# Experts' results added into one row per token by the sending transfers

## The reference

```python
h = _layernorm(x) * (1 + ca) + sa
x = x + ga * attention_stack(h)              # 4 layers, 16 heads of 8
h = _layernorm(x) * (1 + cb) + sb            # 4096 tokens
probs = softmax(h @ router_w + router_b)     # E = 16 experts
vals, idx = top_k(probs, 2); vals = vals / sum(vals)
pos = place of the pair among those of its expert; within = pos < C   # C = 640
expert_inputs[idx, pos] += h * within
expert_outputs = (silu(xe @ w_gate) * (xe @ w_up)) @ w_down           # F = 176
output = (expert_outputs[idx, pos] * vals * within).sum over the token's 2 pairs
x = x + gb * (h + shared_mlp(h) + output)
```

## Time and profile before

| | |
|---|---|
| median of three runs | 1048.8 us (1045.79 to 1053.61) |
| the profiled execution | 1059.5 us |
| its span, first to last instruction | 1057.7 us |
| TensorE busy | 866.6 us (82%) |
| GpSimd busy | 734.4 us (69%) |
| VectorE busy | 729.1 us (69%) |
| ScalarE busy | 561.4 us (53%) |
| GpSimd, five sends for each of 16 experts (L633) | 80 x 0.96 us |
| DMA moved | 115.19 MB |

### The profile page before, as it was taken

The page is one execution under the profiler, slowest core; times in us unless marked ns, Lnnn a source line. Parts: engine busy times, 40 slices in busy tenths (PEclk is TensorE's granted clock), DMA queues, the critical chain, the costliest instruction groups (busy, mean ns, idle before and its releaser), DMA issues.

```text
span 1057.7 us, 10906 instructions
## 1 busy us (share of the span) xinstructions
PE 866.6 (82%) x3053; PEld 429.0 (41%) x3053; DVE 729.1 (69%) x1317; ACT 561.4 (53%) x885; POOL 734.4 (69%) x636
## 2 busy tenths in 40 slices
PE   4389998998999899999999996686643897989750
PEld 2034443433444343444444442244321465666530
DVE  3679998898888889888989898475552432222216
ACT  5358876775767577768787885553311121222110
POOL 3899988997999877898989896436626015545550
PEclk9689999998999899999999998786666787888775
DMA  7835444644636535535353440211211013232317
GB/s 222 237 91 141 121 115 126 168 115 114 180 103 159 148 102 135 150 80 143 96 136 104 113 126 1 59 41 61 80 53 51 23 31 101 81 94 79 101 35 238
DMA packets 89673, 115.19 MB, mean 109 GB/s; under 512 B 12960, under 2 KB 47238, under 8 KB 89614
## 3 DMA queue, kind: packets, MB, share of 16 engines
q1 hardware_dynamic: 80672, 102.87, 35.7%
q0 software_dynamic: 4608, 9.51, 2.7%
q10 hardware_dynamic: 4334, 2.13, 0.7%
HBM read 22.02 MB, written 21.14 MB: 41 GB/s over the span
## 4 chain that ended last, share of the span: by engine, by line
PE 56%; issue 14%; DVE 10%; DMA 5%; POOL 5%; SPq 3%; ACT 3%; another core or an unknown queue 3%; DVEq 0%; POOLq 0%; ACTq 0%
PE ps L1149 7%; PE ps L642 6%; PE ps L1075 6%; PE ps L1170 4%; PE ps L1130 4%; PE ps L1136 4%; DVE wnum L1526 3%; PE ps L1102 3%; PE ps L1116 3%; PE ps L1110 2%; POOL kv L951 2%; PE ps L1100 2%; PE ps L1127 2%; DMA kv<-expert_in_scratch 2%
## 5 line engine op out<-in xcount | busy, mean ns | idle before, releaser
L951 POOL TENSOR_TENSOR kv<-kv,kT 128x1024 f32<-128x1024 f32 x128 | 306.3, 2394 | 63.4 <-DMA kv<-vT 46.6
L1520 DVE TENSOR_TENSOR_SCAN kvsum<-kv,ps 128x256 f32<-128x256 f32 x256 | 166.9, 673 | 9.9 <-POOL kv L956 9.9
L956 POOL TENSOR_TENSOR kv<-kv 128x512 f32<-128x512 f32 x128 | 165.9, 1307 | 0.0
L633 POOL DMA_INDIRECT pair_out_scratch<-kv,idx_y x80 | 76.8, 960 | 126.3 <-DVE kv L772 103.2
L1526 DVE TENSOR_TENSOR wnum<-kvsum,ps 128x1024 f32<-128x1024 f32 x128 | 154.2, 1204 | 1.0
L1149 PE MATMUL ps<-u,w 128*128 128x512 f32 x256 | 122.3, 600 | 1.5 <-issue 0.9
L1365 ACT ACTIVATE hT<-ps,bias_h 128x512 f32<-128x512 f32 x128 | 84.6, 690 | 36.8 <-PE ps L1149 36.8
L1075 PE MATMUL ps<-u,wqkv 128*128 128x512 f32 x192 | 96.7, 629 | 5.5 <-ACT u L1281 3.3
L1170 PE MATMUL ps<-wnum,gather_e 128*32 128x512 f32 x512 | 69.2, 613 | 14.0 <-DVE wnum L1526 7.5
L619 POOL DMA_INDIRECT expert_in_scratch<-wnum,scat_u x64 | 62.9, 983 | 20.4 <-issue 17.9
L1149 PEld LDWEIGHTS ps<-u,w 128*128 128x128 f32 x256 | 48.7, 192 | 63.9 <-issue 54.7
(11 more groups left out here) (243 smaller groups left out, 1693.9 us busy)
## 6 DMA issues: line engine op xcount, KB each, us to landing
kv<-vT SPq DMA_DIRECT2D x256, 256.0 KB, 4.3
expert_in_scratch<-room SPq DMA_DIRECT2D x16, 325.0 KB, 4.8
kv<-expert_in_scratch SPq DMA_DIRECT2D x16, 325.0 KB, 2.9
pair_out_scratch<-room SPq DMA_DIRECT2D x16, 256.0 KB, 4.5
wnum<-x SPq DMA_DIRECT2D x16, 256.0 KB, 2.8
kv<-pair_out_scratch SPq DMA_DIRECT2D x8, 512.0 KB, 4.3
x<-in_L_attn_x_dram SPq DMA_DIRECT2D x8, 256.0 KB, 4.3
mod<-mod_scratch SPq DMA_DIRECT2D x1, 2048.0 KB, 9.8
```

The lines of the kernel that those rows point to most:

```text
L633: pool.indirect_dma_start(out=y_dram, out_offset=bass.IndirectOffsetOnAxis(ap=idx_y[:, par, j:j + 1], axis=0), in_=yes[:, par, j * P:(j + ...
L951: pool.tensor_tensor(pair, pair, kT[:, par:par + 1, :].to_broadcast([P, 2, S]), ALU.mult).then_inc(kv_weighed, 1)
L956: pool.tensor_tensor(even_, even_, odd_, ALU.add).then_inc(kv_done, 1)
L1520: dve.tensor_tensor_scan(kvsum[:, i, 1:PAIRS + 1], kv[:, par, i, 0:PAIRS], ps_q[:, 0:PAIRS], 0.0, ALU.add, ALU.bypass).then_inc(kvsum_done, 1)
```

## The change

- `y_dram` has one row per token instead of two (4096), then the rows of the empty places. Both pairs of a token get the same row number: the two iotas make the same numbers, and the third starts at 4096.
- The sends of results are made with an addition (`compute_op=ALU.add`): a row is added to what the row in DRAM holds, zeros or the other expert's result.
- Before its five sends expert e waits on GpSimd until the sends of expert e-1 have landed (for e > 0). The two experts of a token are different, so within one expert's sends each token's row comes once.
- `clear` writes 128 KB instead of 256 KB of zeros a slot into `y_dram`.
- In the final mix the load is one row per token (256 KB), and VectorE multiplies and adds x; the sum of the two pairs is gone.

Everything else is as it was, two line numbers further down behind L632.

```diff
--- before.py
+++ after.py
@@ -52,9 +52,9 @@
 
     XW = D + 2
     xe_dram = nc.dram_tensor("expert_in_scratch", [ROWS + 2 * TOK, XW], F32, kind="Internal").ap()
-    y_dram = nc.dram_tensor("pair_out_scratch", [2 * TOK + ROWS, D], F32, kind="Internal").ap()
+    y_dram = nc.dram_tensor("pair_out_scratch", [TOK + ROWS, D], F32, kind="Internal").ap()
     xe_tiles = xe_dram[0:ROWS, :].rearrange("(e p j) d -> e p (j d)", e=E, p=P)
-    y_rows = y_dram[0:2 * TOK, :].rearrange("(b p r) d -> b p (r d)", b=B, p=P)
+    y_rows = y_dram[0:TOK, :].rearrange("(b p r) d -> b p (r d)", b=B, p=P)
 
     with ExitStack() as ctx:
         def sb(name, shape, dt=F32):
@@ -252,7 +252,7 @@
         hs = wnum_room[:, 0:RING * 2 * NT * XW].rearrange("p (r k n c) -> p r k n c", r=RING, k=2, n=NT)
         YES = TILES * D + 2 * CT * XW
         yes = kv_room[:, YES:YES + 2 * CAP].rearrange("p (a c) -> p a c", a=2)
-        ypair = kv_room[:, 0:TILES * D].rearrange("p (r k n d) -> p r k n d", r=4, k=2, d=D)
+        ysum = kv_room[:, 0:TILES * D // 2].rearrange("p (r n d) -> p r n d", r=4, d=D)
         GROUPS = ((0, 1), (1, 3), (3, 5), (5, 7), (7, 8))
         ROUTE_SLOT = (33, 34, 35, 37, 38)
 
@@ -328,7 +328,7 @@
                 part = b % 4
                 if b >= 4:
                     sp.wait_ge(out_store[part], 16)
-                sp.dma_start(ypair[:, part, :, :, :].rearrange("p k n d -> p (k n d)"), y_rows[b]).then_inc(y_load[part], 16)
+                sp.dma_start(ysum[:, part, :, :].rearrange("p n d -> p (n d)"), y_rows[b]).then_inc(y_load[part], 16)
             for part in range(4):
                 sp.wait_ge(out_store[part], 16 * 2)
             sp.wait_ge(q["xe_zeroed"], 16 * E)
@@ -629,10 +629,12 @@
                 pool.tensor_copy(weight_y[:, par, :], xes[:, par, :, D + 1]).then_inc(q["idx_ready"], 1)
                 pool.wait_ge(q["idx_ready"], 2 * e + 2)
                 pool.wait_ge(q["ye_sb"], e + 1)
+                if e:
+                    pool.wait_ge(y_scat[1 - par], (e + 1) // 2 * (16 * CT))
                 for j in range(CT):
                     pool.indirect_dma_start(
                         out=y_dram, out_offset=bass.IndirectOffsetOnAxis(ap=idx_y[:, par, j:j + 1], axis=0),
-                        in_=yes[:, par, j * P:(j + 1) * P], in_offset=None).then_inc(y_scat[par], 16)
+                        in_=yes[:, par, j * P:(j + 1) * P], in_offset=None, compute_op=ALU.add).then_inc(y_scat[par], 16)
             for e in range(E):
                 scatter_outputs(e, e % 2)
 
@@ -736,7 +738,7 @@
 
             for b in range(B):
                 act.wait_ge(q["out_ready"], b + 1)
-                act.dma_start(out_v[b], ypair[:, b % 4, 0, :, :]).then_inc(out_store[b % 4], 16)
+                act.dma_start(out_v[b], ysum[:, b % 4, :, :]).then_inc(out_store[b % 4], 16)
 
         def dve_shared_hidden(dve, r):
             if r == 0:
@@ -795,11 +797,9 @@
             for b in range(B):
                 part = b % 4
                 dve.wait_ge(y_load[part], 16 * (b // 4 + 1))
-                both = ypair[:, part, 0, :, :]
-                dve.tensor_tensor(both, both, ypair[:, part, 1, :, :], ALU.add).then_inc(q["mix_step"], 1)
-                dve.wait_ge(q["mix_step"], 2 * b + 1)
+                both = ysum[:, part, :, :]
                 dve.tensor_tensor(both, both, wide(mod[:, b:b + 1, 3, :]), ALU.mult).then_inc(q["mix_step"], 1)
-                dve.wait_ge(q["mix_step"], 2 * b + 2)
+                dve.wait_ge(q["mix_step"], b + 1)
                 dve.tensor_tensor(both, both, X[:, tile_rows(b), :], ALU.add).then_inc(q["out_ready"], 1)
 
         block = ctx.enter_context(nc.Block())
@@ -857,7 +857,7 @@
             def clear(e):
                 sp.wait_ge(q["zrow_ready"], e + 1)
                 sp.dma_start(xe_tiles[e], zrow[:, :, :].rearrange("p j c -> p (j c)")).then_inc(q["xe_zeroed"], 16)
-                sp.dma_start(y_dram[e * S:(e + 1) * S, :].rearrange("(p j) d -> p j d", p=P), zrow[:, 0:NT, 0:D]
+                sp.dma_start(y_dram[e * S // 2:(e + 1) * S // 2, :].rearrange("(p j) d -> p j d", p=P), zrow[:, 0:NT // 2, 0:D]
                              ).then_inc(q["y_zeroed"], 16)
 
             for k in range(SLOTS):
@@ -928,9 +928,9 @@
                 pool.tensor_scalar(trash[:, :, :], trash_less[:, :, :], float(ROWS), None, ALU.add).then_inc(consts_ready, 1)
                 for k in range(2):
                     rows_k = iota_i[:, 96 + k * TILES:96 + (k + 1) * TILES]
-                    then(pool.iota(rows_k, pattern=[[2 * NT * P, B], [1, NT]], base=k * NT, channel_multiplier=2 * NT))
+                    then(pool.iota(rows_k, pattern=[[NT * P, B], [1, NT]], base=0, channel_multiplier=NT))
                 pool.tensor_copy(pair_row_v, iota_i[:, 96:96 + 2 * TILES]).then_inc(consts_ready, 1)
-                pool.iota(iota_i[:, 160:160 + E * CT], pattern=[[CAP, E], [1, CT]], base=2 * TOK, channel_multiplier=CT
+                pool.iota(iota_i[:, 160:160 + E * CT], pattern=[[CAP, E], [1, CT]], base=TOK, channel_multiplier=CT
                           ).then_inc(consts_ready, 1)
 
             def label_empty(e):
```

## The result

The changed kernel takes 1076.65 us (median of 4 runs, 1072.95 to 1080.64), before beside it 1051.2: a ratio of 1.0236 (95% interval 1.0152 to 1.0321). Run once more beside other kernels it came to 1.0264 (1.0196 to 1.0333). The forecast was 1042, 0.6% faster; it is 2.4 to 2.6% slower. Every ratio compares fast executions with fast executions of the kernel before from the same set. That kernel's median lay between 1046.6 and 1054.7 us from one set to the next, so whole times are compared within a set only.

The account below looks back on a forecast made before the run. It took the chain through GpSimd's five sends, two copies and a load per expert pair, then the final mix, as bounding. Final mix -7.9, landing and wait +1.2, issue and clears 0: -6.7 us, 1042 us; own range 1037 to 1048, eight-in-ten 1035 to 1066.

Parts of the forecast that it names:

- Issue: GpSimd's time to issue an adding send: taken as no longer than a plain one, 0 us, range 0 to 43.
- 45 d: Cost if each adding send's issue on GpSimd is d us longer, 45 being on the path; d from 0 to 0.96.
- the issue grows: Slower rival at GpSimd's sends before the odd expert's load: 1065 at 0.5 us more each, 1085 at 0.96; chance 0.18.
- Landing: Adding sends land later because the old row is read first: +1.0 us, once before the final loads; range 0.2 to 2.4.
- New wait: GpSimd holds an expert's sends until the previous expert's land: nothing lost in the loop, 0.2 us at expert 15.
- The bound of 4.0: Upper bound in us for landing and new wait together, given as 2.4 + 1.6; the forecast took 1.2.
- The pile-up: Slower rival: DMA engines finish one send's additions before the next's, landing 7 us after the last issue; 1069, chance 0.09.
- Final mix: End, from first y load: halved loads and one sum fewer a row give 18.8 instead of 26.7 us, gain 7.9.
- the turnaround to row 4: Final mix: row 0's store issued at 4.36, row 4's load out at 7.5 and landing at 10.4 us.
- rows 4 to 7 then follow every 1.42: Final mix: after row 4's load lands, the last four rows follow at VectorE's pace, 1.42 us each, to 16.0.
- Clears: Sixteen y clears on GpSimd halve: taken as 0 us, bound 0 to -1.
- the high end: Upper limit for the adding send's issue on GpSimd: descriptor list doubles, 0.96 us more a send, 43 us in all.

Follow-up runs that it names:

- e1: Kernel before with the adding sends alone: two rows per token, no new wait, old final mix; 1078.1 us, ratio 1.031.
- e9: Kernel before, plain sends, with one idle addition on GpSimd behind each send to hold it longer; ratio 1.0168.
- e2: Kernel before with the new wait alone, plain sends into two rows per token; ratio 1.0017.
- e12: Changed kernel with GpSimd's copies for the next expert put ahead of the sends and eight final-mix buffers instead of four; 1057.2 us, ratio 1.0121.
- e4: Changed kernel with each expert's fourth and fifth send cut to 64 and 32 rows; run once, 1075.4 us.
- e8: Kernel before with each expert's fourth and fifth send cut to 64 and 32 rows; run once, 1050.0 us.

## Why the prediction was wrong

- *Issue.* The step that failed is "I take 0, the value of the only rows of this operation". The term was 45 d with d between 0 and 0.96; d is 0.593, so 26.7 us. The rows of plain sends said nothing of another form of the instruction, and the whole range from 0 to 43 us deserved more than 0.11 for over 1%. The count of 45 came close (49 and 52 by e1 and e9, with the slower clock behind the waits in them): put into the sum, 26.7 makes +20.0 of -6.7, against 24.4 measured. The rival "the issue grows" is what happened.
- *Landing.* 3.4 us from the last issue to the load, against 2.28 + 1.0. Of the 1.1 us more, 0.6 is the longer issue, which the 45 d hold already. The landing itself cost 0.5, half of the 1.0 taken. The packets of the software queue rose from 4608 to 13568, that is 144 a send instead of 32, and the last send's now keep the engines busy for about 0.9 us (1049.7 to 1050.6) instead of a quarter. In the changed kernel the queue's row is:

```profile
q0 software_dynamic: 13568, 9.51, 6.8%
```

- *New wait.* Nothing with plain sends (e2), and 0.3 us at the last expert against 0.2. Within the loop the forecast of nothing is not shown for adding sends: the wait holds back the sends of five experts before the last by 0.2 to 0.5 us, the loads behind them have nothing left to spare, and e1, without the wait, was 1.1 us shorter, which is within what two executions differ by. The bound of 4.0 also left out the 0.9 that the forecast itself allowed for nine semaphore conditions; no run shows a price for them. The pile-up did not come: 0.9 us of transfers fit between issues 1.86 apart.
- *Final mix.* 6.1 us, forecast 7.9, inside its bounds (6.0 to 10.3). The first landing (2.67 for 2.9) and the turnaround to row 4 (5.2 from row 0's store to row 4's sum for 6.0) were shorter than taken. What failed is "rows 4 to 7 then follow every 1.42": they came at 1060.38, 1062.95, 1065.51 and 1067.53, 2.0 to 2.6 us apart, waiting 1.2 us for three of the loads and 0.6 for the last. e12 shows what the buffers withheld: 16.8.
- *Clears.* Not tried alone. The first send of results comes 852.6 to 863.5 us after the start in the six profiles with half clears and 848.5 to 867.5 in the eight with whole ones, so no gain is seen.
- *What was left out.* 26.7 + 0.5 + 0.3 = 27.5 of the 30.5 us. Three things stand for the rest and were not measured apart: TensorE's clock (with the even experts' loads late too, since 5 x 0.59 is more than the 2.0 us that they had to spare, its hidden matmuls take 76.4 us in all instead of 69.9), the loads' later landing, and the wait in the loop. The forecast had none of the clock, though its own rows showed it: behind a wait for a load the transposes took 1.33 us, at 992.84 only 0.77. Nor were the odd experts' waits all of 2.9 to 3.1 us; one of the seven was 1.56 and one 2.58.

The sentence of the Trainium skill on which the high end rested (GPSIMD Engine Reference, When to use GPSIMD: one core writes read descriptors, the other write descriptors) gets no support as the main price: if doubled lists are what the rows' share is, they come to 0.15 of the 0.59 us. The rows' share did double, but no run shows what GpSimd does in it, nor in the fixed 0.44.

## What to carry to other kernels

A flag on an instruction makes another instruction: where its price multiplies a count on the chain, zero is a bound and not an estimate, and a chance must stand on the whole range. Before pricing a longer step, ask why it is on the chain at all: here two tiny copies stood behind five sends in one engine's queue, and moving them was worth more (2.6 to 3.0%) than the 10 us, 1%, that the shortest end of all (e12) saved. Cut profiles at fixed points of the program rather than compare spans, when executions of one kernel differ by more than the change.

## What was not expected of the hardware

- An indirect send of 128 rows of 512 bytes holds GpSimd 0.96 us plain and 1.55 us with addition; by three sizes (e4, e8) about 0.83 us + 1.0 ns a row against 1.27 us + 2.2 ns a row.
- With addition a send of 128 rows is 144 packets instead of 32. The DMA engines' share among the experts rose from 0.30 to 0.49 while they moved fewer bytes a second (86 and 79 GB/s). The loads beside them landed 0.3 us later, some 2 us of the 30 by my estimate.
- Behind a wait of 3 us TensorE is granted 0.50, and twelve matmuls take 5.02 instead of 3.63 us; in the changed kernel the transposes take 1.33 us instead of 0.77 behind waits of 1.4 us too. Reordering GpSimd's copies saved 25 to 27 us among the experts, where TensorE's seven waits for loads alone came to 18.9.
